# State-space stage of a four-part model: order of ScalarE's long tasks, dt and softplus in a hand-written schedule, mean square on VectorE

## The reference

```python
h  = rmsnorm(layernorm(x), rms1_w)
xm, z = split(h @ W_in.T)                       # 512 channels each
xc = silu(causal_conv4(xm) + conv_b)
dt, Bm, Cm = split(xc @ W_xproj.T, [64, 80])    # 64, 16, 16
delta = softplus(dt @ W_dt.T + b_dt)
# 16 states n for each channel:
#   h_n[t] = exp(delta[t] * A_n) * h_n[t-1] + delta[t] * Bm[t, n] * xc[t]
#   y[t]  += Cm[t, n] * h_n[t]
y = (y + D_skip * xc) * silu(z)
x = res + y @ W_out.T
# then the row scale rsqrt(mean(x * x) + 1e-6) of the second rmsnorm, the router's logits, the experts
```

## Time and profile before

| | |
|---|---|
| median of 3 runs | 2460.20 us (2458.91 to 2461.51) |
| the profiled execution | 2457.92 us |
| its span | 2456.2 us |
| mean granted TensorE clock | 0.866 of full speed |
| busy, share of the span | PE 78%, VectorE 68%, ScalarE 48%, GpSimd 60% |
| 180 to 300 us of the span | VectorE 107.9, ScalarE 88.1, GpSimd 113.6, PE 96.0 of 120 us busy |

### The profile page before, as it was taken

The page is one execution under the profiler, slowest core; times in us unless marked ns, Lnnn a source line. Parts: engine busy times, 40 slices in busy tenths (PEclk is TensorE's granted clock), DMA queues, the critical chain, the costliest instruction groups (busy, mean ns, idle before and its releaser), DMA issues. The chain is left out here.

```text
span 2456.2 us, 35764 instructions
## 1 busy us (share of the span) xinstructions
PE 1920.1 (78%) x10252; PEld 1469.4 (60%) x10253; DVE 1676.1 (68%) x3193; ACT 1185.9 (48%) x2021; POOL 1483.1 (60%) x1118
## 2 busy tenths in 40 slices
PE   6787878796979787876599999907877784799970
PEld 2445454554555554644499999904655664699970
DVE  1789898989899898985644444436734897644438
ACT  2776767777777767773222222226632441111112
POOL 1799999898989898984133333335622420355532
PEclk9797979797989888887699999958987896799995
DMA  4111111111111010112411111142000014122226
GB/s 125 36 35 40 36 40 35 40 35 41 37 38 38 29 45 31 44 36 82 165 48 47 48 48 47 41 139 77 9 18 11 9 35 163 44 70 70 68 66 191
DMA packets 76781, 138.63 MB, mean 56 GB/s; under 512 B 10370, under 2 KB 47874, under 8 KB 75859
## 3 DMA queue, kind: packets, MB, share of 16 engines
q1 hardware_dynamic: 62994, 99.67, 12.3%
q0 software_dynamic: 13632, 37.24, 4.9%
HBM read 104.86 MB, written 32.01 MB: 56 GB/s over the span
## 5 line engine op out<-in xcount | busy, mean ns | idle before, releaser
L779 DVE TENSOR_TENSOR_SCAN a_hs<-a_dA,a_carry,a_hs 128x512 f32<-128x512 f32 x512 | 628.9, 1267 | 78.2 <-POOL a_hs L396 38.7
L396 POOL TENSOR_TENSOR a_hs<-a_u,a_b_bc 128x1024 f32<-128x1024 f32 x258 | 626.4, 2431 | 0.4
L921 PE MATMUL a_h_ps<-k_ident,a_hs 128*128 128x128 f32 x2064 | 326.6, 307 | 147.1 <-DVE a_acc L742 79.1
L921 PEld LDWEIGHTS a_h_ps<-k_ident,a_hs 128*128 128x128 f32 x2064 | 268.0, 158 | 270.8 <-DVE a_acc L742 75.5
L551 ACT ACTIVATE a_dA<-a_delta,a_a_neg 128x512 f32<-128x512 f32 x512 | 350.8, 688 | 31.2 <-DVE a_hs L779 29.3
L408 POOL TENSOR_TENSOR a_acc<-a_acc,a_part 128x512 f32<-128x512 f32 x242 | 317.7, 1313 | 59.7 <-ACT a_part L565 58.7
L565 ACT ACTIVATE a_part<-a_h_ps,a_c_tok 128x512 f32<-128x512 f32 x242 | 165.9, 686 | 193.6 <-PE a_h_ps L921 186.4
L1221 POOL DMA_INDIRECT expert_rows<-m0e_ys,k_pair x71 | 79.1, 1114 | 232.4 <-DVE m0e_ys L1277 217.9
L855 PE MATMUL a_fx<-a_hT,a_w_x 128*128 128x512 f32 x432 | 201.9, 599 | 2.2 <-ACT a_halo L487 1.4
L742 DVE SCALAR_TENSOR_TENSOR a_acc<-a_h_ps,a_c_tok,a_acc 128x512 f32<-128x512 f32 x242 | 176.1, 728 | 30.7 <-PE a_h_ps L921 30.7
L1287 DVE TENSOR_TENSOR m0e_hT<-m0e_gs,m0e_u 128x512 f32<-128x512 f32 x70 | 48.2, 689 | 190.9 <-ACT m0e_gs L1240 190.9
(11 more groups left out here) (420 smaller groups left out, 3793.2 us busy)
## 6 DMA issues: line engine op xcount, KB each, us to landing
a_b_bc<-b_rows SPq DMA_DIRECT2D x132, 256.0 KB, 3.1
c_y<-expert_rows SPq DMA_DIRECT2D x16, 512.0 KB, 5.7
q_y<-expert_rows SPq DMA_DIRECT2D x16, 512.0 KB, 5.9
norm_rows<-a_x SPq DMA_DIRECT2D x9, 512.0 KB, 3.2
m0w_up<-in_m_up SPq DMA_DIRECT2D x1, 4096.0 KB, 12.5
m0w_gate<-in_m_gate SPq DMA_DIRECT2D x1, 4096.0 KB, 22.4
m0w_down<-in_m_down SPq DMA_DIRECT2D x1, 4096.0 KB, 31.9
c_xl<-in_L_attn_x SPq DMA_DIRECT2D x8, 512.0 KB, 3.5
```

The lines of the kernel that those rows point to most:

```text
L396: pool.tensor_tensor(hs[n % NBUF][:, half, :], u[s][:, half, :], b_bc[:, n % NBUF:n % NBUF + 1, :].broadcast_to([P, 2, T]), ALU.mult).then ...
L779: dve.tensor_tensor_scan(hs[k][:, c, :], dA[c][:], hs[k][:, c, :], carry[:, hf, c, n:n + 1], ALU.mult, ALU.add).then_inc(s_scan, 1)
L921: last = pe.transpose(hT_ps[j % 2][:, c * P:(c + 1) * P], hs[(n - 1) % NBUF][:, c, j * P:(j + 1) * P], ident[:])
```

## The change

- `LONG_END`: in states 8, 10 and 11, ScalarE issues factor(n+1,3) ahead of the tasks of `END_ACT` instead of behind them.
- `dt` is run in two halves: two of its four channel chunks after turn 3 of state 9, two after turn 1 of state 10.
- Softplus is half a state later: exp from the middle of state 11 to its end, round from the end of 11 to the middle of 12, ln from the end of 12 to the middle of 13, and on VectorE fix from the middle of 12 to its end, sub from the end of 12 to the middle of 13, add from there to the end of 13. GpSimd writes u in state 14, behind its products and adds, instead of 13.
- The mean square of the row scale (square, epsilon, sum) is computed by VectorE in two operations; GpSimd keeps the power.

```diff
-                 11: ["d2", "d3"], 12: ["o0"], 13: ["z0"], 14: ["z3"], 15: ["r"]}
+                 10: ["dt.2", "dt.3"], 11: ["d2", "d3"], 12: ["o0"], 13: ["z0"], 14: ["z3"], 15: ["r"]}
...
-                7: ["xc2.3", "xc3.0"], 8: ["xc3.2", "xc3.3"], 9: ["dt"], 10: ["d0", "d1"], 11: ["ct"], 12: ["o1"], 13: ["z1", "z2"],
+                7: ["xc2.3", "xc3.0"], 8: ["xc3.2", "xc3.3"], 9: ["dt.0", "dt.1"], 10: ["d0", "d1"], 11: ["ct"], 12: ["o1"], 13: ["z1", "z2"],
...
-        MID_ACT = {1: ["norms"], 2: ["f1"], 10: ["dt"], 11: ["d2", "d3", "exp"], 13: ["z0"], 14: ["x1", "z2", "z3"]}
+        MID_ACT = {1: ["norms"], 2: ["f1"], 10: ["dt"], 11: ["d2", "d3"], 12: ["round"], 13: ["z0", "ln"], 14: ["x1", "z2", "z3"]}
...
-                   11: ["round", "ct"], 12: ["ln"], 13: ["z1"], 14: ["g0", "g1"], 15: ["rows"]}
+                   11: ["exp", "ct"], 13: ["z1"], 14: ["g0", "g1"], 15: ["rows"]}
+        LONG_END = (8, 10, 11)
...
             def rms(tile0, nth):
 
-                pool.wait_ge(s_mv2, nth(1))
-                pool.tensor_tensor(ms[:], mv2[:, :, 0], mv2[:, :, 0], ALU.mult).then_inc(s_ms, 1)
-                pool.wait_ge(s_ms, nth(3) + -2)
-                pool.tensor_tensor(ms[:], ms[:], eps_rms[:], ALU.add).then_inc(s_ms, 1)
-                pool.wait_ge(s_ms, nth(3) + -1)
-                pool.tensor_tensor(ms[:], ms[:], mv2[:, :, 1], ALU.add).then_inc(s_ms, 1)
-                pool.wait_ge(s_ms, nth(3))
+                pool.wait_ge(s_ms, nth)
                 pool.tensor_tensor(R2[:, bass.ds(tile0, TJ)], ms[:], halfneg[:, :, 0], ALU.pow).then_inc(s_rr, 1)
...
-                        if n == 14:
-                            rms(tile0, lambda per_: lin(U, per_, per_))
-                        if n == NS - 3:
+                        if n == NS - 2:
                             pool.wait_ge(s_xc, lin(F, 1, 1))
                             pool.wait_ge(s_free[side("xc3")], count("xc3", U))
                             for q in range(2):
                                 front_u(F, 1 - hf, q)
+                        if n == 14:
+                            rms(tile0, lin(U, 1, 1))
...
                         factor(U, n + 1, 2, there)
+                        if n in LONG_END:
+                            factor(U, n + 1, 3, there)
                         for name in END_ACT.get(n, []):
                             task(name)
-                        factor(U, n + 1, 3, there)
+                        if n not in LONG_END:
+                            factor(U, n + 1, 3, there)
...
                     last = dve.bn_aggr(mv2[:, j, :], st2[:, j, :])
-                last.then_inc(s_mv2, 1)
+                link(last, padded=True)
+                link(dve.tensor_tensor(ms[:], mv2[:, :, 0], mv2[:, :, 0], ALU.mult))
+                dve.scalar_tensor_tensor(out=ms[:], in0=ms[:], scalar=EPS_RMS, in1=mv2[:, :, 1],
+                                         op0=ALU.add, op1=ALU.add).then_inc(s_ms, 1)
...
-                        if n == 12:
-                            softplus_fix(F, 1 - hf)
                         if n == 13:
-                            softplus_add(F, 1 - hf)
+                            softplus_sub(F, 1 - hf)
                         scan(2)
                         scan(3)
                         summed(U, n, 2, here)
                         summed(U, n, 3, here)
                         if n == 12:
-                            softplus_sub(F, 1 - hf)
+                            softplus_fix(F, 1 - hf)
                             dve.wait_ge(s_full["Y"], count("o0", U))
                             dve.wait_ge(s_xn, lin(U, 1, 1))
                             residual(0, fy, tile0).then_inc(s_free["Y"], 1)
+                        if n == 13:
+                            softplus_add(F, 1 - hf)
...
-                    for c in range(EC):
+                    for c in range(EC) if part_ is None else (part_,):
```

More of the change, by code:

```diff
@@ L165, in mamba_phase @@
         ms = m.sb("ms", [P, TJ])
-        eps_rms = m.sb("eps_rms", [P, TJ])
         x1 = m.sb("x1", [P, TJ, D])
@@ L200, in mamba_phase @@
         s_pw = m.sem("shift")
-        s_mv2 = m.sem("moments2")
         s_ms = m.sem("meansq")
@@ L293, in mamba_phase @@
         N_PREP = 1 + EC + 7
-        PER_D = 2 * (2 + 2)
+        PER_D = 2 * (2 + 5)
         SCANNED, TURNED, KEPT = EC, 8, 2 * NS
@@ L363, in _ @@
             pool.memset(halfneg[:], -0.5).then_inc(s_const, 1)
-            pool.memset(eps_rms[:], EPS_RMS).then_inc(s_const, 1)
             pool.memset(z[1][:], 0.0).then_inc(s_prep, 1)
@@ L368, in _ @@
             pool.sem_inc(s_add, NO)
-            pool.wait_ge(s_const, 2)
+            pool.wait_ge(s_const, 1)
             def front_power(F, s):
@@ L444, in _ @@
                 add(end, 0, j, 1)
-            rms(TILES - TJ, lambda per_: per_ * (2 * NB + 1))
+            rms(TILES - TJ, 2 * NB + 1)
         @block.scalar
```

## The result

| | before | changed |
|---|---|---|
| median | 2460.18 us | 2478.11 us (12 runs) |
| ratio | | 1.0072, 95% interval 1.0057 to 1.0087 |
| the profiled execution | 2457.92 us | 2473.53 us |
| its span | 2456.2 us | 2471.7 us |
| mean granted TensorE clock | 0.866 | 0.862 |

The change costs 0.7%. The forecast was 2450.8 us with a range up to 2466: the sign is wrong and the time lies outside the range.

A forecast was written before the change was run, and what follows sets the result against it. GpSimd was taken as the bound, losing 10.8 us a half to waits, locks and small operations. -1.45 a half, -11.6 over eight, another 0.4 at the end, less 1.9 to 2.7 for TensorE's clock: net -9.4, 2450.8 us, range 2436 to 2466.

The forecast's parts named there:

- Steps 1 to 3: States 8 to 12: earlier factors, dt halves and later exp remove GpSimd waits of 0.33, 0.39 and 1.78, 2.5 us.
- Step 4: End of state 12: fix passes at the add's end, then alternates with GpSimd, +1.0 twice; done at 307.8.
- Even: Rival, chance 0.23: round ends after 303.4, first fix waits 2.3 for product(13,1); about -0.2 a half, 2459 us.
- z0 (step 4): TensorE: the wait of 4.24 ahead of z0 shrinks to about 2, so z0 takes nearer 2.0 than 3.78.
- Step 5: Ln moved: 1.18 wait goes; 6.0 from z0's eviction to add(13,3), where GpSimd waits 1.3 instead of 3.42.
- the walk: The prediction's queue-by-queue timing of one half with the trace's durations; it put product(0) at 336.45 against 337.89.
- step 7: State 14: add(14,3) needs scan, sum, turn and ScalarE tasks, so GpSimd has a new wait of 3.4 us.
- Step 6: End of state 13: add pair alternates with a busy GpSimd, +1.0 twice, lasting to 324.0 instead of 322.1.
- Step 8: Rest of the half: mean square on VectorE taken as 0.5, covered by its slack; GpSimd's 0.9 goes.
- Slower: Rival, chance 0.17: VectorE ends last, its two small operations each caught 2.35 behind GpSimd; +1.3 a half, 2471 us.

The follow-up runs named there:

- b_order: Kernel before with the last factor of states 8, 10 and 11 ahead of ScalarE's tasks and dt in halves, nothing else; 2434.84 us, ratio 0.9906.
- a_self: Changed kernel plus a GpSimd wait for its own last instruction, ahead of the second product of state 12; 2450.59 us, ratio 0.9971.
- a_gate: Changed kernel plus a GpSimd wait for the fix's first half, ahead of its second add of state 12; 2444.73 us, ratio 0.9943.
- a_met: Changed kernel plus a GpSimd wait ahead of the second product of state 12, for an add long done; 2472.88 us, ratio 1.0065.
- the two blocks: Probes ahead of the kernel before, VectorE freed after varied GpSimd run lengths; its first instruction took 1.7 to 2.8 us after 3, 16.33 to 19.84 after 15.
- the first block: Probe ahead of the kernel before: VectorE pairs of several sizes and operand kinds beside ten GpSimd instructions; both inputs in SBUF 5.47 us, 128x4 pair 1.28.

## Why the prediction was wrong

1. **Steps 1 to 3 (order, dt, exp) were right and too small.** The waits of 0.33, 0.39 and 1.78 are gone in the changed kernel; in `b_order` the third stays in three halves, at 0.31 to 1.51. Without exp's move the order gives 25 us, 3.2 a half, where I gave the three steps 2.5.
2. **Step 4 is the one that failed.** "passes at the add's end. Then they take turns" took the gap of 0.12 at 304.78 and the turns of the earlier trace rows for what the lock always does. In the kernel before, GpSimd waits for a part just there and at 301.20. In the changed kernel it comes to the fix after more than 40 instructions without a pause in seven of eight halves, and steps 1 to 3 and the fix's later place together leave no add held by its part at the boundary in five of them: there it keeps the pair, and the first fix takes 6.3 to 11.0 us where the prediction had 2.1 (0.9 of waiting and its own 1.2). Letting it in is worth 25 to 28 us (`a_self`, by ratios or medians). That the pair is kept, and that a pause ends it, is shown by `a_gate`, `a_self` against `a_met`, and the two blocks. The condition that the prediction named for Even was met as well: the round ends after product(13,1) has begun (437.24 against a fix issued at 438.39), so even the third half has 129.73, where Even said 129.5.
3. **z0 (step 4).** Its wait did shrink from 4.24 to 2.04, as forecast, and it still took 3.67, near TensorE's slower level (granted clock 0.55 from 443.5 to 447.3). That a wait of about 2 gives about 2.0 had no row behind it when it was predicted, and here it puts the 1.7 us straight into the wait at add(13,3). In `a_gate` it does come out: 1.99 in six of eight halves (clock 1.00), behind 0.44 to 2.26 of idle time. So the idle time just ahead does not settle the level alone (2.04 to 2.17 gave 3.54 to 3.67 in the changed kernel), and what does stays open.
4. **Step 5, 6.0 from z0's eviction to add(13,3), was right** (447.85 to 453.84). But GpSimd arrives 0.8 behind that eviction where the walk had 4.7: counted from the start of product(13,1), the eviction comes 3.0 later than walked (fix and z0), and GpSimd 0.9 earlier, as the first sub costs it nothing. So the wait is 5.20 and not 1.3, and the 3.4 of step 7 is nought in this half. In `a_gate` the 1.3 comes out as forecast, and the 3.4 in its size.
5. **Step 6 was right in kind**: in the third half the add pair takes 3.42, as GpSimd is busy; in the halves with a long fix, where it has stopped, 2.34 to 2.35.
6. **Step 8 was mis-sized.** The small operations were put at 0.5 in all; they take 2.2 in the third half (0.98 + 1.18) and 3.4 at 593.14, 0.32 where GpSimd stands (`a_gate`). The rival Slower had this price, and it is not what made the change slower: the order and the softplus alone, with the mean square where it was, give 2482.63.
7. **What the prediction took from the Trainium skill.** The Trainium skill (SBUF — State Buffer, SBUF: two separate sides) says that while one of the two has the shared pair the other "fully blocks". The rows agree, down to 128x4 (1.20 beside a GpSimd instruction in the first block). The prediction used this for who waits within one instruction and had no term for who gets the pair at the next boundary. For table loads the row decided again: 1.28 each in the changed kernel. The Trainium skill (ScalarE: Activation LUTs, What ACT_TABLE_LOAD costs) gives 2.66 for a switch.

The sum itself (2450.8) is what the changed kernel gives once nobody is kept out: 2450.59 with the pause, 2444.73 with the gate. The first is luck: from the first writing of u to the last, `a_self` takes 907.6 us, only 2.2 less than the kernel before, where the walk had 10 less; the rest of its gain lies in the first half and at the ends. `a_gate` takes 897.2, 12.6 less, and is the nearer to the walk, though points 1, 3, 4 and 6 are misses of both signs.

What stays open: whether a part that comes just in time is by itself enough to let VectorE in (the 12 cases say so, no run isolates it), and what tells the one add at 0.19 from those at up to 0.20. Nor is it known whether instructions or microseconds count in the run: at 2.34 and 1.26 in turns, less their overlaps, 13 instructions are some 23.5 us and 15 some 27.

## What to carry to other kernels

A gap that you remove from one engine may be another engine's only way in. Where VectorE and GpSimd both work from SBUF, list for each large VectorE instruction the GpSimd instructions since its last pause; if there are more than a dozen, and GpSimd's next instruction there is not one that is just being released by a wait, put a wait of GpSimd for its own last instruction shortly ahead of the place, which costs about 0.1 us. And time the parts of a bundle one by one: here one part was worth 25 us, and the bundle cost 18. Their prices did not add up, so time the pairs too.

## What was not expected of the hardware

- The shared access of VectorE and GpSimd to SBUF is handed over at every boundary only as long as GpSimd has run briefly (or, by the 12 cases above, where its next instruction has only just been released). After 13 instructions without a pause VectorE's first took 2.3 us, after 15 it took 16 to 20, that is until GpSimd stopped; GpSimd itself was not slowed at all in the blocks (2.34 and 1.26 throughout). A pause of 0.08 us starts this anew.
- One input in PSUM frees a VectorE instruction from this (0.69 and 0.68 of 128x512 beside a busy GpSimd); one input alone does not, if it is in SBUF (tensor_scalar, 4.48 for two).
- GpSimd's jump at the loop's turn takes its sequencer 2.5 to 3.6 us in all these kernels. It costs nothing where enough work is queued (the kernel before), 1.4 to 1.5 us in the changed kernel, and up to 2.1 us where the last instruction before it waits for a part.
